# Graph transformer layer pair: where the self-loops, folds and row transposes are done

## Chip, cores and metric

One core of a Trainium2 chip runs the whole program. The metric is the device time of one execution in microseconds; the shown time is the median of three runs. TensorE (PE) runs at one of two clocks, 1.2 or 2.4 GHz, as the chip grants them; the granted clock is given as a share of the higher one. DVE is the vector engine, ACT the scalar engine, POOL is GpSimd, SP the engine that here only issues DMAs.

## What is computed

N = 3125 nodes of width 128, 103,125 directed edges (100,000 drawn, both ways, and 3125 loops), sorted by destination; the layer adds another self-loop for every node. Two layers follow each other, after `h = relu(layernorm(x))`. The reference, cut:

```python
xn = _layernorm(x, ln1_g[l], ln1_b[l])
pos = xn @ Wpos[l] + bpos[l] + deg[:, None] * Wdeg[l][0] + bdeg[l]
xp = xn + pos
q, k, v = xp @ Wq[l] + bq[l], xp @ Wk[l] + bk[l], xp @ Wv[l] + bv[l]     # 8 heads of 16
att = clip(einsum('ehd,ehd->eh', q[dst], k[src]) / scale, -50, 50)       # nan -> 0
ex = exp(att - m[dst]); alpha = ex / segment_sum(ex, dst)[dst]
aggr = segment_sum(v[src] * alpha, dst)
x = x + (aggr @ Wo[l] + bo[l])
x = x + (gelu(_layernorm(x, ...) @ W1[l] + b1[l]) @ W2[l] + b2[l])
```

## The kernel before

Nodes lie in 25 blocks of 128 (partition = node in its block). There are two orders of the blocks: the natural one, and the ranked one (blocks by how many tiles of edges they have), in which both layers work. `NAT` are the 7 batches of four natural blocks (the last has one), `CHUNKS` the 9 chunks of ranked blocks (seven of three, two of two). Edges come in 806 tiles of 128, taken in 202 groups of up to four a layer (6 "seam" groups that touch two blocks a tile, 196 main ones).

**Prelude.** A histogram in 16 steps (`hist_step`) counts degrees: DVE makes one-hot tiles, PE multiplies them. Between its steps PE does other small work: it folds the position weights into Wq, Wk, Wv of both layers (`fold_bias`, `fold_positions`, two matmuls of 384 columns in each, "u" and "fold"), transposes the normalised input (`turn_nat`) and the rows of edge indices (`turn_rows`: k 0 and 1 the destinations, 2 and 3 the sources). Then it makes keys and values of 25 blocks in 13 pairs (`keys_values`), which DVE copies to `kv_nat` (adding the degree term) and SP stores to a table in HBM; then the queries of 7 batches (`queries`). For each batch DVE copies the queries out (`queries_nat`), computes the self-loops' scores (`self_scores`: five instructions, lines 1455 to 1459), and, with ACT, splits the queries into three bf16 parts (`q_first_nat`, `q_rest_nat`, `q_second_nat`, `q_third_nat`; two buffers `q_parts`). ACT takes the exponential (`loop_exp_nat`), DVE multiplies it with the values (`loop_values_nat`). SP moves each block's three parts to its rank in `qp` (L622, one DMA of 96 KB a block). `degT` and `degR` put the degrees in ranked order, at the end of the queries.

POOL gathers rows of the table by edge (L755, one indirect DMA a tile, 128 KB) into a ring of 8 groups, `kvr`. `kv_nat` lies in that ring, so in the first groups POOL waits for the batches of self-loops (`elif 1 <= n <= NATS: pool.wait_ge(s_agg0, n)`).

**Edge phase**, for each layer: in iteration n DVE runs `edge_iteration` (product q*k, L1522; the sums of group n-2 into `agg`, L1549; message of n-1, L1540; scores L1526; clipping L1530 to L1535; one-hot of n+2, L1515), PE `edge_q(n+1)` (L992) and `edge_sum(n-1)` (L1005), ACT the exponentials and the transposed one-hots. One iteration is called a slot here; it lasts from one L1522 to the next. PE's bank 2 holds one group's queries, so `edge_q(n+1)` waits for the product of n.

When a chunk's edges are done, its dense work (`dense_parts`) is spread over the next slots after `BASE[c]` (32, 56, 81, 105, 129, 154, 178, 195, 203): DVE in slot 0 `attention_norm`, 2 `add_to_x`, 4 and so on; in the first layer also the next layer's q, k, v from slot 13 on, whose own self-loops are made from them (`loop_scores` in slot 15, `loop_values` in slot 17). Each engine runs its parts behind its own part of the edge iteration. SP sorted the first layer's finished self-loops into rank order by 25 DMAs in slot 4 (`rank_loops`, L629), and loads the input again from slot 8 (`load_x0`).

Of the kernel before, what the change touches and what calls it, by code (L numbers as in the profile page):

```python
# [113 lines left out]
ROWS_AFTER = {1: (0,), 3: (1,), 5: (2,), 6: (3,)}  # L114
# [6 lines left out]
SP_OUT, SP_TABLE = 10, 15  # L121
SLOTS = BASE[-1] + DVE_Q3 + 1
# [73 lines left out]
def turn_numbers():  # L196
# [9 lines left out]
    for l in range(L):  # L206
        use(0, l, "u", 3 + 2 * l)
    for l in range(L):
        use(0, l, "fold", 7 - l)
# [8 lines left out]
    for c in range(NATS):  # L218
        use(0, c, "q", (1, 4, 5, 6, 7, 3)[c % 6])
    for phase in range(1, L + 1):  # L220
# [29 lines left out]
def build(nc, x_in, src_flat, src_tiles, dst_tiles, dst_last, weights, out):  # L250
    with ExitStack() as ctx:
# [39 lines left out]
        loops_nat = sb("loops_nat", [P, BLOCKS, AGG])  # L291
# [73 lines left out]
        x0 = x_nat = loops_nat[:].rearrange("p b c -> p (b c)")[:, 0:NP].rearrange("p (b c) -> p b c", c=D)  # L365
# [3 lines left out]
        spare = spare[:, 2 * HE:2 * HE + 8 * SC * P].bitcast(F32)  # L369
        step_dst, step_src = (spare[:, k * SC * P:(k + 1) * SC * P].bitcast(I32) for k in range(2))  # L370
        step_dst_f, step_src_f = (spare[:, k * SC * P:(k + 1) * SC * P] for k in (2, 3))
# [7 lines left out]
        spare = hT[:].rearrange("p f c -> p (f c)")  # L379
        wposT = spare[:, 0:L * D].rearrange("p (l c) -> p l c", l=L)  # L380
        wdeg_wide = spare[:, L * D:2 * L * D].rearrange("p (l c) -> p l c", l=L)
        counts = spare[:, 4 * D:4 * D + HI]
# [65 lines left out]
        s_loops_ranked = sem("s_loops_ranked")  # L448
# [78 lines left out]
        def turn_no(phase, c):  # L527

            return NATS + (phase - 1) * NCH + c + 1

# [37 lines left out]
        def _(sp):  # L568
# [55 lines left out]
            def rank_loops():  # L624

                sp.wait_ge(s_agg0, NATS)
                for b0, nb in NAT:
                    for j, r in enumerate(read_block_ranks(ENG.SP, b0, nb)):
                        sp.dma_start(loops[:, bass.ds(r, 1), :], loops_nat[:, b0 + j:b0 + j + 1, :]).then_inc(s_loops_ranked, 16)  # L629

            def load_x0():

                sp.wait_ge(s_loops_ranked, 16 * BLOCKS)
# [24 lines left out]
            for l in range(L):  # L658
                for s in range(SLOTS):
# [15 lines left out]
        def _(pool):  # L675
# [65 lines left out]
            for n in range(L * GROUPS):  # L741
# [9 lines left out]
                elif 1 <= n <= NATS:  # L751
                    pool.wait_ge(s_agg0, n)
# [5 lines left out]
        def _(pe):  # L758
# [26 lines left out]
            def fold_bias():  # L785
# [12 lines left out]
                for l in range(L):  # L798
                    pe.wait_ge(s_wdeg, l + 1)
                    pe.matmul(use(0, l, "u")[:, 0:3 * D], wdeg_wide[:, l, :], w[l][:, W_QKV:W_QKV + 3 * D], start=True, stop=True).then_inc(full(0, l, "u")[0], 1)  # L800

            def fold_positions():
                pe.wait_ge(*read(0, 0, "posT"))
                for l in range(L):
                    pe.matmul(use(0, l, "fold")[:, 0:3 * D], wposT[:, l, :], w[l][:, W_QKV:W_QKV + 3 * D], start=True, stop=True).then_inc(full(0, l, "fold")[0], 1)
# [50 lines left out]
            for k in range(HSTEPS):  # L856
# [6 lines left out]
                elif k == 3:  # L863
                    fold_bias()
                elif k == 4:
                    turn_ranks()
                elif k == 6:
                    fold_positions()
# [10 lines left out]
            for l in range(L):  # L879
                pe.wait_ge(*read(0, l, "fold"))  # L880
# [12 lines left out]
            pe.wait_ge(s_deg, 1)  # L893
            pe.transpose(degT_ps, deg[:, 0, :], ident[:]).then_inc(s_degT_ps, 1)
            pe.wait_ge(s_degT, 1)
# [796 lines left out]
```

## Time and profile before

| | |
|---|---|
| median of 3 runs | 2920.66 us (2920.16 to 2921.53) |
| the profiled execution: time, span | 2918.08 us, 2916.4 us |
| start of keys and values on PE | 108.66 us |
| first gather of layer 1 | 149.74 us |
| first and last issue of the DMAs to qp | 158.88, 191.69 us |
| first edge matmul, first product | 195.25, 199.85 us |
| first product of layer 2 | 1562.8 us |
| mean granted clock of PE | 0.64 |

The difference between the execution's time and its span, 1.7 us, lies around the program. A time of the table is read from the start of the span. Everything before 195.25 us is the prelude; the remaining 2721 us are the two edge phases and their tails.

### The profile page before, as it was taken

What the parts mean: (1) busy time and instruction counts of PE and PEld (TensorE: products, weight loads), DVE (VectorE), ACT (ScalarE), POOL (GpSimd) and SP (SyncE); (2) the same over time, 40 slices, a digit from 0 to 9 for tenths busy, and PEclk for the clock granted to TensorE, in tenths of its full rate; (3) what the DMA queues carried; (4) which work ended last, traced back from release to release, by engine and by line L of the source; (5) the groups of instructions that cost most, each with busy time, mean ns of one, the idle gap of its engine ahead of it and who ended that gap; (6) DMA issues with size and microseconds to landing.
All of it is one profiled execution on the core that took longest, in us unless ns stands there. A gap on an engine that the chain in (4) does not pass through costs nothing.

```text
span 2916.4 us, 39090 instructions
## 1 busy us (share of the span) xinstructions
PE 1839.7 (63%) x9908; PEld 1461.3 (50%) x9908; DVE 1729.1 (59%) x5116; ACT 945.9 (32%) x2192; POOL 1570.4 (54%) x1669
## 2 busy tenths in 40 slices
PE   7956566666666656666673665666565666656666
PEld 6635444544545545454552544555454545545545
DVE  7365565656666666566672555555556656565565
ACT  7122224242333323242442222323232323323233
POOL 5055555555555555555524555565555555555651
PEclk8556657575756657565665755756566665666576
DMA  3144333333333333333322333333333333333331
GB/s 88 58 126 144 107 98 94 111 97 102 103 109 101 103 95 105 103 96 109 102 60 77 112 103 93 104 107 100 107 91 107 103 106 96 108 100 106 106 95 34
DMA packets 123531, 289.01 MB, mean 99 GB/s; under 512 B 31524, under 2 KB 57056, under 8 KB 123328
## 3 DMA queue, kind: packets, MB, share of 16 engines
q0 software_dynamic: 77824, 212.31, 25.4%
q1 hardware_dynamic: 45504, 74.20, 7.7%
q8 instruction: 102, 1.67, 0.2%
q14 instruction: 101, 0.83, 0.1%
HBM read 272.16 MB, written 8.38 MB: 96 GB/s over the span
## 4 chain that ended last, share of the span: by engine, by line
another core or an unknown queue 33%; DVE 29%; issue 17%; PE 17%; DVEq 2%; ACT 2%; SPq 1%; POOL 0%; DMA 0%; ACTq 0%; POOLq 0%
DVE agg L1549 13%; PE bank L1005 5%; PE bank L992 5%; DVE onehot L1515 3%; DVE prod L1522 3%; PE bank L781 2%; DVE attc L1535 2%; DVE msg L1540 1%; DVEq L557 1%; DVE att L1526 1%; DVE attnan L1530 1%; PE bank L842 1%; PE bank L947 1%; PE bank L770 1%
## 5 line engine op out<-in xcount | busy, mean ns | idle before, releaser
L755 POOL DMA_INDIRECT kvr<-kv_table,srcidx x1612 | 1526.2, 947 | 1227.3 <-DVE msg L1540 677.5
L992 PE MATMUL bank<-qp,onehotT 128*128 x4992 | 690.2, 269 | 706.8 <-DVE prod L1522 383.3
L1005 PE MATMUL bank<-msg,onehot 128*128 128x136 f32 x3328 | 817.7, 420 | 310.6 <-DVE msg L1540 310.4
L992 PEld LDWEIGHTS bank<-qp,onehotT 128*128 128x128 bf16 x4992 | 497.9, 103 | 955.7 <-issue 841.4
L1005 PEld LDWEIGHTS bank<-msg,onehot 128*128 128x128 f32 x3328 | 706.7, 304 | 336.2 <-DVE msg L1540 333.7
L1549 DVE TENSOR_TENSOR agg<-agg,bank 128x136 f32 x1628 | 471.6, 290 | 517.2 <-remote 478.2
L1184 ACT ACTIVATE bank<-attc 128x32 f32<-128x32 f32 x404 | 81.2, 201 | 1743.3 <-DVE attc L1535 1481.2
L1522 DVE TENSOR_TENSOR prod<-kvr,bank 128x512 f32<-128x512 f32 x404 | 276.1, 683 | 413.8 <-remote 350.9
L1175 ACT ACTIVATE apart<-relT,minus_p 128x512 bf16<-128x512 bf16 x416 | 293.8, 706 | 0.5
L1515 DVE TENSOR_TENSOR onehot<-bank,rel 128x512 f32<-128x512 f32 x416 | 282.9, 683 | 0.5
L1540 DVE TENSOR_TENSOR msg<-kvr,bank 128x512 f32<-128x512 f32 x404 | 274.4, 679 | 0.7 <-ACT bank L1184 0.5
L1526 DVE TENSOR_REDUCE att<-prod 128x32 f32<-128x512 f32 x404 | 273.6, 677 | 0.1
L1179 ACT ACTIVATE onehotT<-apart 128x512 bf16<-128x512 bf16 x416 | 261.9, 629 | 13.1
L1531 DVE TENSOR_SCALAR attc<-att 128x32 f32<-128x32 f32 x404 | 96.8, 240 | 0.0
L1419 DVE TENSOR_TENSOR x<-x,bank 128x384 f32<-128x384 f32 (+1 forms) x36 | 18.9, 524 | 118.3 <-PE bank L770 55.5
L1187 ACT ACTIVATE msg<-attc 128x32 f32<-128x32 f32 x404 | 86.0, 213 | 0.0
L781 PE MATMUL bank<-kvr 128*128 128x100 bf16 x416 | 76.9, 358 | 11.3 <-DVE kvr L1225 11.3
L1535 DVE COPY_PREDICATED attc<-attnan,zeros 128x32 f32<-128x32 uint8 x404 | 75.1, 186 | 0.0
L1530 DVE TENSOR_TENSOR attnan<-att 128x32 uint8<-128x32 f32 x404 | 74.0, 183 | 0.1
L781 PEld LDWEIGHTS bank<-kvr 128*128 128x128 bf16 x416 | 60.0, 145 | 27.4 <-DVE kvr L1225 12.2
L947 PE MATMUL bank<-w,hT 128*128 128x128 f32 x400 | 68.9, 325 | 3.2 <-issue 2.6
L1184 ACT ACT_TABLE_LOAD x51 | 65.4, 1283 | 0.9
(209 smaller groups left out, 1018.0 us busy)
## 6 DMA issues: line engine op xcount, KB each, us to landing
relT<-rel_table SPq DMA_DIRECT2D x104, 512.0 KB
kvr<-kv_table,srcidx POOLq DMA_INDIRECT x1612
kv_table<-qkv SPq DMA_DIRECT2D x25, 128.0 KB
kv_table<-kvr SPq DMA_DIRECT2D x12, 256.0 KB, 2.1
qp<-hT SPq DMA_DIRECT2D x25, 96.0 KB
loops<-loops_nat SPq DMA_DIRECT2D x25, 68.0 KB
w<-weights SPq DMA_DIRECT2D x2, 840.0 KB, 7.4
loops<-x_in SPq DMA_DIRECT2D x5, 320.0 KB, 5.6
```

The source lines that it names most:

```text
L755: pool.indirect_dma_start(kvr[:, n % RING, j, :], None, kv_table[l], bass.IndirectOffsetOnAxis(ap=srcidx[:, step:step + 1], axis=0)).then_ ...
L781: mm = pe.matmul(counts_ps, oh_low[:, buf, :, :, t].rearrange("p i n -> p (i n)"), oh_high[:, buf, :, :, t].rearrange("p i n -> p (i n)"), ...
L992: mm = pe.matmul(bank[2][:, j * D:(j + 1) * D], onehotT[:, m % OHT, j, :], qp[:, bass.ds(ranks[j + h], 1), part, :].rearrange("p a c -> p ...
L1005: mm = pe.matmul(sum_ps(n, k), onehot[:, m % OH, j, :], msg[:, n % 2, j, :], start=(m, j) == of[0], stop=(m, j) == of[-1])
L1175: act.activation(apart[:], relT[:, m // BODY % 2, r, :], ACT.Abs, bias=minus_p[:]).then_inc(s_apart, 1)
L1179: act.activation(onehotT[:, m % OHT, :, :].rearrange("p j e -> p (j e)"), apart[:], ACT.Relu, bias=1.0, scale=-1.0).then_inc(s_ohT, 1)
L1184: act.activation(ex, attc[:, n % 2, :], ACT.Exp).then_inc(s_ex, 1)
L1515: dve.tensor_tensor(onehot[:, m % OH, :, :], iota_ps.unsqueeze(1).broadcast_to([P, G, P]), rel[:, row:row + G].unsqueeze(2).broadcast_to([ ...
L1522: dve.tensor_tensor(prod[:], kvr[:, n % RING, :, 0:D], bank[2][:].rearrange("p (j c) -> p j c", c=D), ALU.mult).then_inc(s_prod, 1)
L1526: dve.tensor_reduce(att[:, n % 2, :], prod[:].rearrange("p j (h d) -> p (j h) d", d=HD), AX, ALU.add).then_inc(s_att, 1)
L1540: dve.tensor_tensor(by_head(msg[:, n % 2, :, 0:D]), by_head(kvr[:, n % RING, :, D:KV]), ex.rearrange("p (j h) -> p j h", h=H).unsqueeze(3) ...
L1549: dve.tensor_tensor(target, target, sum_ps(n, j), ALU.add).then_inc(s_agg, 1)
```

## The change

1. First layer's self-loops: no longer made in natural order in the prelude, but for each ranked chunk c shortly before its `BASE[c]`. SP loads the chunk's keys and values back from the table (`load_loops`, slot -7, one DMA of 128 KB a block), DVE adds up the three bf16 parts of the queries (`loop1_queries`, slot -4, two additions), computes the scores (slot -3), ACT the exponential (slot -3), DVE the product with the values (slot -2). `rank_loops` and POOL's waits for `s_agg0` go.
2. Second layer's "u" and "fold", and the transposes of the destination rows (`turn_rows` 0 and 1), leave the histogram; PE does them behind the queries, ACT and DVE take them up there; the one-hots of groups 0 and 1 are made there too, behind the queries on DVE.
3. `degT` and `degR` are done among the keys and values (PE behind pairs 6 and 8, DVE behind pairs 2 and 4).
4. Buffers: `x_nat` gets its own memory, `loops_nat` goes; `step_dst_f` lies in `msg`, `wposT` and `wdeg_wide` in `xnT`.

```diff
-ROWS_AFTER = {1: (0,), 3: (1,), 5: (2,), 6: (3,)}
+ROWS_AFTER = {5: (2,), 6: (3,)}
+SP_LOOP1, DVE_LOOP1_Q, DVE_LOOP1_SCORES, ACT_LOOP1, DVE_LOOP1 = -7, -4, -3, -3, -2
...
+            def load_loops(c):
+                b0, nb = CHUNKS[c]
+                blocks = read_perm(ENG.SP, b0, nb)
+                if c >= 2:
+                    sp.wait_ge(s_table[buffer(1, c)], stored(1, c - 2))
+                    sp.wait_ge(s_agg0, loop_no(1, c - 2))
+                    sp.wait_ge(s_r1, turn_no(1, c - 2))
+                    sp.wait_ge(s_q1, turn_no(1, c - 2))
+                table = kv_table[0].rearrange("(b p) c -> p b c", p=P)
+                for j, b in enumerate(blocks):
+                    sp.dma_start(qkv[:, buffer(1, c), j:j + 1, D:3 * D], table[:, bass.ds(b, 1), :]).then_inc(s_loop1_kv, 16)
...
-                    if (l, s) == (0, BODY):
-                        rank_loops()
-                    elif (l, s) == (0, 2 * BODY):
+                    if (l, s) == (0, 2 * BODY):
                         load_x0()
                     for c, at in parts_at(s, LATE_SP):
+                        if l == 0 and at == SP_LOOP1:
+                            load_loops(c)
...
-                elif 1 <= n <= NATS:
-                    pool.wait_ge(s_agg0, n)
...
             for i in range(2, len(KV_PAIRS)):
                 keys_values(i)
+                if i == 6:
+                    pe.wait_ge(s_deg, 1)
+                    pe.transpose(degT_ps, deg[:, 0, :], ident[:]).then_inc(s_degT_ps, 1)
+                elif i == 8:
+                    pe.wait_ge(s_degT, 1)
+                    pe.matmul(degR_ps, degT, placed[:], start=True, stop=True).then_inc(s_degR_ps, 1)
             for c in range(NATS):
                 queries(c)
+            for k in range(2):
+                turn_rows(k)
+            for l in range(1, L):
+                fold_degree(l)
+                fold_positions(l)
...
             def attention_norm(phase, c):
                 if l == 0:
+                    dve.wait_ge(s_loop1, c + 1)
...
+            def loop1_queries(c):
+                nb, u = CHUNKS[c][1], buffer(1, c)
+                q = qkv[:, u, 0:nb, 0:D]
+                dve.tensor_tensor(q, blocks_of(qp[:, :, 2, :], c), blocks_of(qp[:, :, 1, :], c), ALU.add).then_inc(s_loop1_sum, 1)
+                dve.wait_ge(s_loop1_sum, c + 1)
+                dve.tensor_tensor(q, q, blocks_of(qp[:, :, 0, :], c), ALU.add).then_inc(s_loop1_q, 1)
...
             for c in range(NATS + 1):
                 if c < NATS:
-                    b0, nb = NAT[c]
                     queries_nat(c)
-                    self_scores(q_nat[:, c % 2, 0:nb, :], kv_nat[:, b0:b0 + nb, 0:D], b0, nb)
                 if c >= 1:
-                    loop_values_nat(c - 1)
                     q_third_nat(c - 1)
                 if c < NATS:
                     q_rest_nat(c)
+            for k in range(2):
+                dve.wait_ge(*read(0, k, "rows"))
+            edge_onehot(0)
+            edge_onehot(1)
+            for l in range(1, L):
+                fold_positions(l)
+                dve.wait_ge(*read(0, l, "u"))
```

## Rows read from the trace of the kernel before

**Rows 1.** The page's busy time by engine, whole span.

```profile
PE 1839.7 (63%) x9908; PEld 1461.3 (50%) x9908; DVE 1729.1 (59%) x5116; ACT 945.9 (32%) x2192; POOL 1570.4 (54%) x1669
```

**Rows 2.** Stretches of the prelude: bounds, length, busy time by engine, clock, DMA share, GB/s.

```profile
50.00:109.00 59.00, 58.75 (x314) 47.85 (x313) 35.60 (x29) 19.82 (x56) 15.12 (x6) 0.59 0.18 51
109.00:147.00 38.00, 38.00 (x83) 16.13 (x82) 11.68 (x31) 5.78 (x11) 0.00 (x0) 0.50 0.22 76
147.00:195.00 48.00, 24.15 (x78) 15.19 (x77) 34.75 (x89) 10.38 (x22) 29.66 (x30) 0.50 0.48 139
```

**Rows 3.** Timeline of PE in the prelude: start, us, line, tiles, records.

```profile
39.15 2.91 PE L800 MATMUL bank<-w,hT 128*128 128x384 f32 x4
...
56.45 2.78 PE L805 MATMUL bank<-w,hT 128*128 128x384 f32 x4
...
84.15 1.06 PE L824 MATMUL bank<-ident,qp 128*128 128x128 f32 x4
...
91.32 0.85 PE L824 MATMUL bank<-ident,qp 128*128 128x128 f32 x3
...
191.32 0.62 PE L896 MATMUL bank<-placed,xn 25*128 25x25 f32 x2 [20.79 <-issue]
```

**Rows 4.** Timeline of DVE from the queries to the first product.

```profile
147.45 2.48 DVE L1515 TENSOR_TENSOR onehot<-bank,rel 128x512 f32<-128x512 f32 x4
150.56 1.12 DVE L1590 SCALAR_TENSOR_TENSOR qkv<-u_deg,deg,bank 128x128 f32<-128x128 f32 x4 [0.63 <-PE bank L770]
...
158.07 0.68 DVE L1605 TENSOR_TENSOR hT<-qres,hT 128x512 bf16<-128x512 f32 x1
...
199.85 0.69 DVE L1522 TENSOR_TENSOR prod<-kvr,bank 128x512 f32<-128x512 f32 x1 [7.68 <-remote]
```

**Rows 5.** Timeline of SP: all the DMAs to qp, then single batches.

```profile
158.88 33.30 SPq L622 DMA_DIRECT2D qp<-hT  x25
...
158.88 2.54 SPq L622 DMA_DIRECT2D qp<-hT  x4
...
176.07 5.80 SPq L622 DMA_DIRECT2D qp<-hT  x4
...
188.78 2.42 SPq L622 DMA_DIRECT2D qp<-hT  x4
```

**Rows 6.** Timeline of POOL: the first gathers of layer 1.

```profile
149.74 0.99 POOL L755 DMA_INDIRECT kvr<-kv_table,srcidx  x1 [42.88 <-DMA kv_table<-kvr]
...
158.42 1.15 POOL L755 DMA_INDIRECT kvr<-kv_table,srcidx  x1 [3.94 <-DVE loops_nat L1611]
```

**Rows 7.** DVE groups by form: count, busy us, mean ns, idle before.

```profile
L1444 DVE TENSOR_TENSOR qres<-qkv,qp 128x384 f32<-128x384 f32 x7 | 3.8, 549 | 0.0
...
L1458 DVE TENSOR_SCALAR loop_att<-loop_att 128x24 f32<-128x24 f32 x7 | 1.9, 266 | 0.2
...
L1444 DVE TENSOR_TENSOR qres<-qkv,qp 128x256 f32<-128x256 f32 x2 | 0.8, 420 | 0.0
```

**Rows 8.** Timeline of DVE, two slots with edge work alone.

```profile
540.74 0.68 DVE L1522 TENSOR_TENSOR prod<-kvr,bank 128x512 f32<-128x512 f32 x1
...
546.18 0.69 DVE L1522 TENSOR_TENSOR prod<-kvr,bank 128x512 f32<-128x512 f32 x1 [1.72 <-remote]
550.59 0.30 DVE L1549 TENSOR_TENSOR agg<-agg,bank 128x136 f32 x1 [3.72 <-remote]
...
553.54 0.68 DVE L1522 TENSOR_TENSOR prod<-kvr,bank 128x512 f32<-128x512 f32 x1
```

**Rows 9.** Timeline of DVE, a long slot with chunk 2's normalisation behind it.

```profile
732.05 0.69 DVE L1522 TENSOR_TENSOR prod<-kvr,bank 128x512 f32<-128x512 f32 x1 [1.77 <-issue]
...
739.41 0.58 DVE L1409 TENSOR_TENSOR agg<-agg,loops 128x408 f32<-128x408 f32 x1
...
740.84 0.69 DVE L1522 TENSOR_TENSOR prod<-kvr,bank 128x512 f32<-128x512 f32 x1
...
744.85 0.69 DVE L1522 TENSOR_TENSOR prod<-kvr,bank 128x512 f32<-128x512 f32 x1 [0.38 <-PE bank L992]
```

More of the change, by code:

```diff
@@ L205, in turn_numbers @@
     use(0, 0, "bias", 4)
[L206 to L209, printed above, removed]
+    use(0, 0, "u", 3)
+    use(0, 0, "fold", 7)
     use(0, 0, "biasT", 4)
@@ L219, in turn_numbers @@
         use(0, c, "q", (1, 4, 5, 6, 7, 3)[c % 6])
+    for k in range(2):
+        use(0, k, "rows", 4 + k)
+    use(0, 1, "u", 6)
+    use(0, 1, "fold", 7)
     for phase in range(1, L + 1):
@@ L797, in fold_bias, with fold_degree, fold_positions @@
                 mm.then_inc(full(0, 0, "bias")[0], 1)
[L798 to L802, printed above, removed]
+            def fold_degree(l):
+                pe.wait_ge(s_wdeg, l + 1)
+                claim(0, l, "u")
+                pe.matmul(use(0, l, "u")[:, 0:3 * D], wdeg_wide[:, l, :], w[l][:, W_QKV:W_QKV + 3 * D], start=True, stop=True).then_inc(full(0, l, "u")[0], 1)
+            def fold_positions(l):
                 pe.wait_ge(*read(0, 0, "posT"))
-                for l in range(L):
-                    pe.matmul(use(0, l, "fold")[:, 0:3 * D], wposT[:, l, :], w[l][:, W_QKV:W_QKV + 3 * D], start=True, stop=True).then_inc(full(0, l, "fold")[0], 1)
+                claim(0, l, "fold")
+                pe.matmul(use(0, l, "fold")[:, 0:3 * D], wposT[:, l, :], w[l][:, W_QKV:W_QKV + 3 * D], start=True, stop=True).then_inc(full(0, l, "fold")[0], 1)
             def turn_bias():
@@ L878, in _ @@
             pe.wait_ge(s_bias3, 16 * PARTS)
-            for l in range(L):
-                pe.wait_ge(*read(0, l, "fold"))
+            pe.wait_ge(*read(0, 0, "fold"))
             keys_values(0)
@@ L1066, in _, with rows_out @@
             act.copy(bias_parts[:], bank[TURN[0, 0, "biasT"][0]][0:PARTS * L * RC, 0:D]).then_inc(read(0, 0, "biasT")[0], 1)
+            def rows_out(k):
+                act.wait_ge(*full(0, k, "rows"))
+                cols = slice(k % 2 * 4 * P, min(SC, (k % 2 + 1) * 4) * P)
+                act.copy((rel, srcidx)[k // 2][:, cols], bank[TURN[0, k, "rows"][0]][:, 0:cols.stop - cols.start]).then_inc(read(0, k, "rows")[0], 1)
             for c in range(NATS):
@@ L1072, in _ @@
                 for k in ROWS_AFTER.get(c, ()):
-                    act.wait_ge(*full(0, k, "rows"))
-                    cols = slice(k % 2 * 4 * P, min(SC, (k % 2 + 1) * 4) * P)
-                    act.copy((rel, srcidx)[k // 2][:, cols], bank[TURN[0, k, "rows"][0]][:, 0:cols.stop - cols.start]).then_inc(read(0, k, "rows")[0], 1)
+                    rows_out(k)
             act.wait_ge(s_deg_in, 1)
@@ L1142, in dense_parts @@
                     b0, by = CHUNKS[c][0], blocks_by(c)
+                    if phase == 1 and at == ACT_LOOP1:
+                        loop1_exp(c)
                     if at == ACT_OUT:
@@ L1316, in position_bias, with fold_positions @@
                 dve.tensor_tensor(bias_col[:, :, R_QKV:R_QKV + 3], bias_col[:, :, R_QKV:R_QKV + 3], added, ALU.add).then_inc(read(0, 0, "bias")[0], 1)
[L1318 to L1322 removed]
+            def fold_positions(l):
+                dve.wait_ge(*full(0, l, "fold"))
+                dve.tensor_tensor(w[l][:, W_QKV:W_QKV + 3 * D], w[l][:, W_QKV:W_QKV + 3 * D], bank[TURN[0, l, "fold"][0]][:, 0:3 * D], ALU.add).then_inc(read(0, l, "fold")[0], 1)
             dve.wait_ge(s_last, 16)
@@ L1365, in _ @@
             dve.wait_ge(s_deg, 1)
-            for l in range(L):
-                dve.wait_ge(*read(0, l, "u"))
+            dve.wait_ge(*read(0, 0, "u"))
             for i, (b0, nb) in enumerate(KV_PAIRS):
@@ L1576, in _ @@
             dve.wait_ge(s_iota_ps, 1)
-            for k in range(2):
-                dve.wait_ge(*read(0, k, "rows"))
-            edge_onehot(0)
-            edge_onehot(1)
             def queries_nat(c):
```

116 lines of the change are left out of this document (69 added, 47 removed).

## The prediction

> **What bounds the kernel now.** I read the page first. PE is busy 63% of the span and DVE 59% [rows 1], so no engine bounds the whole, and the change must be read by stage: the prelude (to 195 us) and the two edge phases.
>
> In the prelude, the stretches show PE without a gap: busy 58.75 of 59.00 us from 50 to 109, and 38.00 of 38 from 109 to 147 [rows 2]. There PE sets the end, and a matmul taken out is worth its own time. From 147 to 195 no engine is full (PE 24.15 of 48 us). The timeline of DVE shows the first batch's third part made at 158.07, and the timeline of SP shows its 25 DMAs to `qp` beginning right then, at 158.88, and taking 33.3 us [rows 4, 5]. The first product comes at 199.85, after 7.68 us of idle time, about 8 us behind the last of these DMAs. So here SP's queue sets the end, 1.33 us a block. This rate is not constant: a batch of four takes 2.54 us at the start, 2.42 near the end, and 5.80 in between. POOL gathers from 149.74 on, pauses for 3.94 us until 158.42 because of a batch of self-loops, and then gathers on [rows 6]. The slow batch lies deep in that second stretch of gathers, so I read the slow rate as gathers and `qp` transfers contending.
>
> In the edge phase slots alternate. The timeline of DVE shows a short slot, 540.74 to 546.18 (5.44 us, with 1.72 of idle time at its end), and a long one, 546.18 to 553.54 (7.36 us, with 3.72 of idle time in it): 12.80 us for two [rows 8]. DVE has 5.4 us of idle time in such a pair, and waits for PE in both places.
>
> **Part 1, less in the histogram.** "u" and "fold" of both layers take 2.91 and 2.78 us [rows 3]; the second layer's halves are 1.45 and 1.39. The two transposes of destination rows take 1.06 and 0.85, overlapped with their neighbours by about 0.2 each, so 1.5 together. DVE's one-hot tiles are not late for this: it is busy only 35.60 of the 59 us [rows 2]. Sum: keys and values begin 4.3 us sooner. The same work comes back behind the queries (PE 1.45 + 1.39 + 1.9 us, ACT's copies, DVE's 2.48 us of one-hots and a fold of 0.5). PE idles 20.79 us there [rows 3], DVE 7.68 [rows 4], so I cost it at nothing. If `qp` arrived 7 us sooner than I say, about 4 us of it would come onto the path.
>
> **Part 2, `degT` and `degR` among the keys and values.** They are three matmul records on an engine that is full there. `degR` takes 0.62 [rows 3] and the transpose no more than a quarter of 1.06 to 0.4; I take 0.8 us together (bounds 0 and 1.0). DVE waits for them behind pair 2 and again behind pair 4, until PE has done pairs 6 and 8. What queues behind it is copies and SP's stores, and it has 26 of 38 us free [rows 2] to catch up before pair 12. The last store, and so the first gather, moves by PE's shift alone: -4.3 + 0.8 = -3.5 us.
>
> **Part 3, no self-loops in the prelude.** The queries are full 3.5 us sooner. DVE then has 1.12 us of copies and two passes before the first third part, without the five score instructions (about 2 us) and `loop_values`. Its 2.48 us of one-hots ended just before the queries were there (0.63 idle), so moving those gives nothing. I count 147.0 for the first queries, two rounds DVE to ACT and back, and the second batch's copy 3.8 us behind the first (PE's pace): first third part ready at about 152.7, against 158.75. SP starts 6 us sooner.
>
> But POOL no longer pauses: it starts at 146.2 and runs 32 gathers back to back, to about 188. Before, SP's first batches met a queue of gathers that had just begun; now the gathers are 6.5 us ahead when SP starts. What do 25 issues cost then? Bounds: 0.64 us each, the first batch of [rows 5], 16 us in all, and then DVE and PE set the pace; and 1.93 (5.80 over three intervals) until the gathers end near 188, then 0.64. The second gives about 18 + 7 blocks with the loads of ranks between, last issue at 198. Before it was 1.33. I take 1.5 us a block, between before's mean and the slow row, as more of the 25 lie under gathers: 37.8 us, last issue at 190.5 against 192.2, a gain of 1.7 us. The expected 6 us are mostly given back.
>
> The Trainium skill bears on this: DMA: Bandwidth & Descriptors, section "SWDGE vs HWDGE vs iDMA", says that gathers and SP's DMAs run on the same 16 DMA engines, which take turns between the queues. The trace agrees in kind (2.54 and 5.80 us for the same batch). Were the turns equal in bytes, half of the 139 GB/s of [rows 2] would carry a block of 98 KB in 1.4 us; that estimate would end the 25 at 187.8 and the sum would be 2.7 us lower.
>
> **Part 4, self-loops in the edge phase.** A chunk of three blocks adds to DVE two additions, the product, the reduction and the values at 0.55 each, and 0.18 + 0.27 + 0.19 of small ones [rows 7]: 3.4 us over three slots (1.1, 1.8, 0.55). A chunk of two has five at 0.42 and small ones: 2.6. In all 7 x 3.4 + 2 x 2.6 = 29 us.
>
> What of it shows? In a short slot 1.72 us of idle time lie exactly where these parts run [rows 8]. In a long slot nothing is free at that place, but chunk 2's normalisation (1.4 us) was put there: the slot lasts 8.79 us (732.05 to 740.84) and the next 4.01, together 12.80, the same pair [rows 9]. So one insertion of 1.4 us is free in either slot. Three in a row are more: slots of 1.8 and 0.55 on one side and 1.1 on the other exceed what the pair has by 0 to 1.2 us. I take 0.5 a chunk for the seven: 3.5. Chunk 7's parts fall among chunk 6's QKV work: 0.7. Chunk 8's fall in the last three slots, where no long wait is left before the tail: 2 of its 2.6 us. Sum +6.2 us (bounds -4, as a shifted slot can also shorten a pair, and 29). ACT gains 9 short exponentials and loses 7; its table is the one that the edge exponentials use. Its table load now comes before the first edge exponential, while ACT waits for it. SP's 25 loads replace 25 smaller DMAs and have 3 slots (19 us) to land; what they wait for is chunk c-2's, two dozen slots old. At chunk 8 it is one slot old, and then SP holds back at most a load that is needed 4 slots later.
>
> **The sum.** -1.7 (prelude) + 6.2 (edge) = +4.5 us on the profiled execution's own 2918.1 (span 2916.4 and 1.7 around it): 2922.6. That execution lies 2.6 below the median; on the median it is 2925, +0.15%. A difference of 0.2% (5.8 us) is about what can be told from none here.
>
> **Rivals.**
> - *Faster: SP's queue is freed.* If the `qp` DMAs keep a pace of 1.0 us instead of 1.5, the prelude gains 14 us, and with +4.5 or less from the edge phase the time is about 2911. For it: 2.42 and 2.54 us for batches beside running gathers. Against: 5.80 in the long stretch. It decides from 1.1 us a block down.
> - *Slower: the gathers take the DMA engines.* At 1.93 us a block until they end, the last issue comes at 198, 6 us later than before; 2920.7 + 6 + 6.2 = 2933. It decides from 1.6 us a block up, with the edge cost as I have it.
> - *Slower: DVE's added work shows.* If more than half of the 29 us lands on the path: 2934; all of it: 2948. For it: DVE's next product follows its last part at once in long slots. Against: the pair that did not grow [rows 9].
> - *Nothing moves.* The 3.5 us of PE's shift are hidden in SP's queue, the insertions in idle time: 2921; I hold it as part of the forecast's own range.
>
> **How the numbers follow.** Forecast, between 2915 and 2926.5: 0.38. Faster: 0.27. Gathers: 0.20. DVE's work: 0.15. The predicted time is the first case's, 2925. The range 2909 to 2937 takes in the first three and the lesser half of the last. Faster 0.27, same 0.38, slower 0.35, from these cases; the likeliest one's own range is 2915 to 2926.5.
>
> **What the profile after would show.** Keys and values on PE from 104.4 us, queries from 143.1; the first gather at 146.2; the first DMA to `qp` at 152.7 and the 25 in 38 us; the first edge product at 198 (199.85 before). From there to the first product of layer 2, 1363 us before, 6 us more; the slots at `BASE[c]` -4 to -2 longer, their neighbours shorter. Layer 2 the same. I am wrong if the 25 DMAs take under 28 or over 42 us, or if the edge phase of layer 1 grows by more than 12 us or shrinks: its pattern of short and long slots may settle differently after each chunk, which no row here lets me price.

## The result, and the profile after

The changed kernel took 2931.95 us (median of 6 runs, 2928.52 to 2935.12) against 2921.1 us of the kernel before beside it (6 runs, 2920.16 to 2924.35). The ratio is 1.0035, with a 95% interval of 1.0022 to 1.0047: slower by a third of a per cent, just clear of the 0.2% that counts as no change. The forecast was 2925 us in a range of 2909 to 2937, with "no change" as the likeliest case. The time lies in the range, but on the slower side.

The profiled execution of the changed kernel took 2928.52 us (span 2926.7), 10.4 us more than that of before. Stretches of the prelude, to set beside [rows 2] (the last one is new):

```profile
50.00:109.00 59.00, 58.15 (x305) 46.40 (x303) 34.81 (x27) 18.62 (x52) 14.38 (x12) 0.92 0.19 51
109.00:147.00 38.00, 38.00 (x88) 17.03 (x87) 11.64 (x32) 5.78 (x11) 0.00 (x0) 0.50 0.26 86
147.00:195.00 48.00, 25.54 (x77) 15.52 (x77) 11.15 (x28) 5.57 (x9) 30.78 (x32) 0.50 0.39 112
195.00:211.00 16.00, 3.79 (x26) 2.47 (x24) 7.81 (x17) 4.98 (x9) 0.00 (x0) 0.50 0.36 113
```

Up to 147 us the work takes as long as it did (PE 58.15 and 38.00 us, before 58.75 and 38.00). Only the granted clock of the first stretch differs, 0.92 for 0.59, and PE's busy time there hardly follows it. From 147 to 195 VectorE is busy 11.15 us where it was 34.75. Only part of that is work taken out, and the DMAs moved less as well (112 GB/s for 139): everything waits. The timeline of SP, then of VectorE (to set beside [rows 4, 5]) and of GpSimd (beside [rows 6]):

```profile
153.78 51.48 SPq L637 DMA_DIRECT2D qp<-hT  x25
...
159.00 7.24 SPq L637 DMA_DIRECT2D qp<-hT  x4
```

```profile
148.11 1.12 DVE L1667 SCALAR_TENSOR_TENSOR qkv<-u_deg,deg,bank 128x128 f32<-128x128 f32 x4 [3.15 <-PE bank L789]
...
152.96 0.69 DVE L1682 TENSOR_TENSOR hT<-qres,hT 128x512 bf16<-128x512 f32 x1
...
180.31 1.12 DVE L1667 SCALAR_TENSOR_TENSOR qkv<-u_deg,deg,bank 128x128 f32<-128x128 f32 x4 [20.28 <-remote]
...
193.08 1.12 DVE L1667 SCALAR_TENSOR_TENSOR qkv<-u_deg,deg,bank 128x128 f32<-128x128 f32 x4 [10.13 <-remote]
...
210.78 0.69 DVE L1603 TENSOR_TENSOR prod<-kvr,bank 128x512 f32<-128x512 f32 x1 [3.54 <-PE bank L1020]
```

```profile
147.30 1.00 POOL L774 DMA_INDIRECT kvr<-kv_table,srcidx  x1 [43.40 <-DMA kv_table<-kvr]
148.61 0.95 POOL L774 DMA_INDIRECT kvr<-kv_table,srcidx  x1 [0.31 <-issue]
...
186.58 0.95 POOL L774 DMA_INDIRECT kvr<-kv_table,srcidx  x1 [0.30 <-issue]
```

The reader is to see three things. VectorE makes the first third part from 152.96 on and has it at 153.65 (forecast 152.7), and SP starts right behind it. GpSimd gathers 32 times without a pause, 1.25 us apart. And VectorE twice waits for TensorE's query matmuls, 20.28 and 10.13 us ("remote": a signal came, and no instruction's recorded end lies where it could have sent it). TensorE's own timeline shows the same from its side:

```profile
159.00 0.28 PE L789 MATMUL bank<-bias,ones 3*128 3x128 bf16 x1
...
168.39 0.26 PE L789 MATMUL bank<-bias,ones 3*128 3x128 bf16 x1 [0.86 <-issue]
171.19 0.37 PE L845 MATMUL bank<-ident,msg 128*128 128x128 f32 x1 [2.54 <-issue]
...
186.59 0.37 PE L845 MATMUL bank<-ident,msg 128*128 128x128 f32 x1 [4.53 <-issue]
188.80 0.37 PE L845 MATMUL bank<-ident,msg 128*128 128x128 f32 x1 [1.84 <-issue]
```

The first row is the last matmul of queries 3: it is recorded until 159.3, and VectorE gets them at 180.31. Seven transposes that took 1.06 + 0.85 us before [rows 3] now start 2.1 to 4.9 us apart and wait for nothing that the profile shows. This ends some 6 us after the last gather was issued (186.58). The trace also records when each signal (a semaphore's update) is sent. TensorE's for queries 3 is sent at 180.28. The next six, for queries 4, 5 and 6, both transposed rows and "u", are sent together, from 193.06 to 193.39, although queries 4 are recorded until 163.0.

Where the 10.4 us are: the first edge product comes 10.9 us later (210.78 for 199.85). From there to the first product of layer 2 (1572.15, before at 1562.83) it took 1361.4 us against 1363.0, 1.6 less. From there to the end it took 1.1 more.

### The profile page after: what moved, and what is told of

It is laid out like the page before. It is cut to its first block, busy times and chain, and to the rows that moved or that the text cites. A ratio compares the mean times of both kernels' runs of the same rounds, so it can differ in the third digit from the quotient of the medians.

```text
span 2926.7 us, 39204 instructions
## 1 busy us (share of the span) xinstructions
PE 1855.4 (63%) x9908; PEld 1474.0 (50%) x9908; DVE 1743.2 (60%) x5146; ACT 947.4 (32%) x2194; POOL 1574.6 (54%) x1669
## 4 chain that ended last, share of the span: by engine, by line
another core or an unknown queue 33%; DVE 30%; PE 17%; issue 17%; DVEq 2%; ACT 1%; POOL 0%; SPq 0%; DMA 0%; ACTq 0%; POOLq 0%
DVE agg L1630 13%; PE bank L1033 6%; PE bank L1020 4%; DVE onehot L1596 4%; DVE prod L1603 3%; PE bank L800 2%; DVE attc L1616 2%; DVEq L572 2%; DVE msg L1621 2%; DVE att L1607 1%; DVE attnan L1611 1%; PE bank L863 1%; PE bank L789 1%; DVE xn L1443 1%
## 5 line engine op out<-in xcount | busy, mean ns | idle before, releaser
L1612 DVE TENSOR_SCALAR attc<-att 128x32 f32<-128x32 f32 x404 | 84.5, 209 | 0.0
```

## The experiments

Theory G: the gathers, run back to back, hold up TensorE and what waits for it. Rivals: SP's queue is slow by itself; what was moved behind the queries (row transposes, folds) comes late; the self-loops' work shows in the edge phase; the gathers take the DMA engines by their bytes. Ratios are to the kernel before on the same chip, with 95% intervals. The chips differ: the first four kernels ran beside a kernel before of 2921.8 us (35 runs), the next four of 2879.5 us (17), the last four of 2261.0 us (9). Only ratios are compared across these groups, and the first two groups' with the third only with care. The changed kernel as it is was timed in the first pair alone.

**Gathers paced by third parts.** The place of the removed pause, filled again:

```
                 if n >= RING:
                     pool.wait_ge(s_msg, n - RING + 1)
+                elif 1 <= n <= NATS:
+                    pool.wait_ge(s_q3, n)
```

> The changed kernel, with GpSimd's gathers of groups 1 to 7 each waiting for one more third part of the prelude's query chunks (the place where the kernel before had them wait for the self-loops). Theory G (the 32 gathers, back to back from 147.3 us, hold up SP's 25 DMAs and TensorE's queries): the gaps of 20.3 and 10.1 us before queries 3 and 4 on VectorE go, the 25 DMAs take under 40 us instead of 51, the first edge product comes at 190 to 199 us instead of 210.8, and the time is 10 to 18 us under the changed kernel's: 2912 to 2922, no slower than the kernel before. Rival S (SP's queue is as slow whatever GpSimd does, and TensorE's late work is its row transposes and folds): the first product stays within 3 us of 210.8 and the time within 3 us of the changed kernel's.

2915.14 us, ratio 0.9984 [0.9964, 1.0004]. Its timelines of SP and VectorE:

```profile
153.19 22.92 SPq L637 DMA_DIRECT2D qp<-hT  x25
```

```profile
176.15 2.48 DVE L1598 TENSOR_TENSOR onehot<-bank,rel 128x512 f32<-128x512 f32 x4 [0.64 <-ACT rel L1104]
...
193.27 0.69 DVE L1605 TENSOR_TENSOR prod<-kvr,bank 128x512 f32<-128x512 f32 x1 [14.18 <-remote]
```

and TensorE's for the first product:

```profile
179.40 2.82 PE L1022 MATMUL bank<-qp,onehotT 128*128 x24 [8.61 <-issue]
```

With one pause of 1.87 us after the fourth gather (from 153.33 on they run again) the 25 DMAs take 22.92 us instead of 51.48, with gathers beside them nearly all the time, and none of TensorE's signals up to 170.80 is late. The gathers themselves are a little slower there: from 153.33 to 171.82 they start 1.54 us apart in the mean, for 1.25. Which of the two matters, the pause or the slower pace that followed it, this run can't tell. So SP's queue is not slow by itself, and a shared use of the DMA engines is not what cost 1.33 or 2.06 us a block. The first product comes 17.5 us sooner than in the changed kernel, and the time is 0.5% better than the changed kernel's ratio. But it could have come sooner still: VectorE has done everything at 179.1, TensorE's matmuls for it are recorded from 179.40 to 182.2, and the signal is sent at 193.15, when the string of gathers, 1.25 us apart by then, has ended (its last starts at 190.78). Work behind the queries is no cause either: the same transposes and folds ran from 167.09 to 170.8.

**Gathers after the queries.** The changed kernel with

```
                 if n >= RING:
                     pool.wait_ge(s_msg, n - RING + 1)
+                elif n == 1:
+                    pool.wait_ge(s_q3, NATS)
```

> The changed kernel, with all gathers but the first group's four waiting for the last third part of the queries. Theory G: with no gather beside them the query chunks on VectorE run without a gap and the 25 DMAs keep to SP's own rate; the first edge product comes at 185 to 195 us. The 28 gathers then take 35 us from the last third part on, 5 us a group against 6.4 us of a slot, so that VectorE waits in the first slots once for the second group, some 2 to 6 us; the time is 2908 to 2920. Rival S: the first product stays within 3 us of 210.8, and the time is that of the changed kernel or above it by that wait.

2931.18 us, ratio 1.0032 [1.0013, 1.0051]. The prelude did what theory G said (25 DMAs in 21.46 us, first product at 188.79), the time did not. The timeline of VectorE tells why:

```profile
188.79 0.69 DVE L1605 TENSOR_TENSOR prod<-kvr,bank 128x512 f32<-128x512 f32 x1 [11.31 <-remote]
...
214.16 0.69 DVE L1605 TENSOR_TENSOR prod<-kvr,bank 128x512 f32<-128x512 f32 x1 [22.34 <-remote]
```

and TensorE's for the second of these products:

```profile
189.73 2.85 PE L1022 MATMUL bank<-qp,onehotT 128*128 x24 [9.49 <-issue]
```

I had expected a wait of 2 to 6 us for the data of the second group; its four gathers had been issued by 179, and the trace has their data landed at 182.26. What came late was TensorE again: 28 gathers ran from 174.16 to 208.9, and the second group's queries were recorded from 189.73 to 192.6 and signalled at 214.06. The string had been moved onto the edge phase, and cost there what it had cost in the prelude. This miss says most of the theory's content: it doesn't matter which work of TensorE the gathers lie beside, but that it has something to hand over while they run 1.25 us apart.

**No self-loops in the first layer.** The loads, scores, exponentials and values of `loop1_*` are left out, and in `attention_norm`:

```
-                    dve.wait_ge(s_loop1, c + 1)
-                    dve.tensor_tensor(blocks_of(agg, c), blocks_of(agg, c), blocks_of(loops, c), ALU.add).then_inc(s_looped, 1)
+                    dve.tensor_tensor(blocks_of(agg, c), blocks_of(agg, c), ones[:, 0:1].unsqueeze(2).broadcast_to([P, CHUNKS[c][1], AGG]), ALU.add).then_inc(s_looped, 1)
```

> The changed kernel without the first layer's self-loops: no loads of keys and values by rank, no scores, exponentials and values for them, and a constant 1 is added to the sums in their place (so the first layer's attention lacks its self-loops). The prediction's price of the nine chunks is 6.2 us in all: 2925.7 if the changed kernel runs at 2932, 2922 beside a run at 2928.5. The reading of the two traces (1361.4 us from first product to first product against 1363.0 before) gives at most 2 us. A third, that the 29 us of VectorE work shows in full, gives 29 us less. The first edge product is at 210.8 us in all of them.

2931.2 us, ratio 1.0034 [1.0016, 1.0051], against 1.0035 with the loops: nothing that the medians can tell. First product at 210.63, from there to layer 2 1357.3 us, 4.1 less than the changed kernel.

**Parts 1 and 2 alone.** The kernel before with the second layer's folds and the row transposes behind the queries, the ranked degrees among the keys and values, self-loops and their pacing as before; the edit on TensorE (those on the other engines are left out here):

```
             for i in range(2, len(KV_PAIRS)):
                 keys_values(i)
+                if i == 6:
+                    pe.wait_ge(s_deg, 1)
+                    pe.transpose(degT_ps, deg[:, 0, :], ident[:]).then_inc(s_degT_ps, 1)
+                elif i == 8:
+                    pe.wait_ge(s_degT, 1)
+                    pe.matmul(degR_ps, degT, placed[:], start=True, stop=True).then_inc(s_degR_ps, 1)
             for c in range(NATS):
                 queries(c)
+            for k in range(2):
+                turn_rows(k)
+            for l in range(1, L):
+                fold_degree(l)
+                fold_positions(l)
```

> The kernel before with parts 1 and 2 of the change alone: the second layer's folds and the row transposes 0 and 1 behind the queries, the ranked degrees among the keys and values; self-loops still in block order in the prelude, and GpSimd's gathers paced by them. Theory G: VectorE starts the keys and values 2.7 us sooner, nothing is held up, and the first edge product comes at 196 to 199.5 us against 199.85; the time is 0 to 4 us under the kernel before's 2921. Rival S (what was moved behind the queries is what comes late): the first product comes 5 us or more later than 199.85, and the time is 2926 or more.

2917.24 us, ratio 0.9992 [0.9973, 1.0011]. First product at 196.7 (199.85 before), from there to layer 2 1361.2. Parts 1 and 2 do no harm, with all their work behind the queries, and the rival that blames that work falls. Against the paced kernel above, which has part 3 too: first product 196.7 and 193.3, then 1361.2 and 1366.2.

**A lead of three groups.** If strings of gathers are the cost, the ring should not be filled in one go. The changed kernel with

```
-                if n >= RING:
-                    pool.wait_ge(s_msg, n - RING + 1)
+                if n >= 3:
+                    pool.wait_ge(s_msg, n - 3 + 1)
+                elif n == 1:
+                    pool.wait_ge(s_q3, 2)
+                elif n == 2:
+                    pool.wait_ge(s_q3, NATS - 2)
```

> The changed kernel, with GpSimd's gathers never more than 3 groups (12 gathers) ahead of VectorE's messages instead of 8 (32 gathers), in both layers; groups 1 and 2 of the first layer wait for 2 and 5 third parts of the queries. Theory G (TensorE stands still while gathers run back to back, once they have run for some 12 us): the first edge product comes at 180 to 188 us instead of 193.3 in the kernel whose gathers were paced by third parts alone, and the first slot of the second layer, 35.2 us with 32 gathers in a row, falls to 6 to 15 us. The time is 2870 to 2895. Rival L (the lead of 8 groups is needed: a gather of 4 x 1.25 us and its landing do not fit behind a message that is only 3 slots old): slots of 6.4 us grow, and the time is 2930 or more. Rival S (the second layer's first slot is long for a reason of its own, the last rows of its table or the clock): it stays at 35 us and the time at 2905 to 2915.

2844.56 us against 2879.51, ratio 0.9881 [0.9866, 0.9897]. First product at 181.47. At the second layer's start the kernel before (and the changed one, 35.2 us as well) loses more than in the prelude. The timeline of VectorE in the kernel before:

```profile
1562.83 0.69 DVE L1522 TENSOR_TENSOR prod<-kvr,bank 128x512 f32<-128x512 f32 x1 [7.85 <-remote]
...
1598.04 0.69 DVE L1522 TENSOR_TENSOR prod<-kvr,bank 128x512 f32<-128x512 f32 x1 [32.18 <-remote]
```

The trace tells that the second wait is TensorE's: its signal is sent at 1597.94, while the second group's gathered data have landed at 1562.94. The timeline of TensorE there, and below it that of the kernel with the lead of three:

```profile
1563.77 2.86 PE L992 MATMUL bank<-qp,onehotT 128*128 x24 [4.97 <-DVE prod L1522]
1598.97 2.86 PE L992 MATMUL bank<-qp,onehotT 128*128 x24 [32.34 <-DVE prod L1522]
```

```profile
1531.80 2.83 PE L1024 MATMUL bank<-qp,onehotT 128*128 x24 [3.60 <-DVE prod L1607]
1540.43 2.83 PE L1024 MATMUL bank<-qp,onehotT 128*128 x24 [5.80 <-DVE prod L1607]
```

Before, the first slot lasts 35.2 us under 32 gathers in a row; here 8.6 under 12. That is 26.6 us at the second layer's start and 29.3 in the prelude (210.78 to 181.47). Of these 56 us some 45 arrive at the end (1.0035 to 0.9881 of 2920 us); the profile with narrow gathers, from the same chip and with the full lead, shows where others go: the first layer's edge phase is 1349.4 us here and 1343.6 there, and the second layer to its end 1316.0 and 1331.5, only 15.5 less although the first slot alone is 27.9 shorter (8.6 for 36.5). The short lead has a price of its own in the slots behind. It is smaller than the gain, so the rivals L and S fall, on this chip.

**A lead of four groups.** The same with

```
-                if n >= RING:
-                    pool.wait_ge(s_msg, n - RING + 1)
+                if n >= 4:
+                    pool.wait_ge(s_msg, n - 4 + 1)
+                elif n == 1:
+                    pool.wait_ge(s_q3, 2)
+                elif n == 2:
+                    pool.wait_ge(s_q3, 4)
+                elif n == 3:
+                    pool.wait_ge(s_q3, NATS)
```

> The same with a lead of 4 groups (16 gathers, 20 us in a row at the second layer's start); groups 1, 2 and 3 of the first layer wait for 2, 4 and 7 third parts. Theory G: the second layer's first slot ends some 5 us after the string of 16 gathers, so 12 to 20 us against 6 to 15 with a lead of 3, and the time is 2 to 10 us above that kernel's. Rival L: the longer lead is the faster one. Rival S: both have 35 us there.

2853.57 us, ratio 0.9919 [0.9902, 0.9937], 0.4% above the lead of 3. First product at 182.3, the second layer's first slot 14.2 us. The price goes with the length of the string: 12 gathers 8.6 us, 16 gathers 14.2, 32 gathers 35.2 (36.5 in the one run with 32 on this chip).

**The kernel before with a lead of three groups.**

```
-                if n >= RING:
-                    pool.wait_ge(s_msg, n - RING + 1)
-                elif 1 <= n <= NATS:
+                if n >= 3:
+                    pool.wait_ge(s_msg, n - 3 + 1)
+                if 1 <= n <= NATS:
                     pool.wait_ge(s_agg0, n)
```

> The kernel before with the lead of 3 groups (its waits for the self-loops kept). Theory G: its prelude has pauses already, so the first edge product comes at 193 to 200 us against 199.85; the second layer's first slot falls as in the changed kernel, and the time is 2890 to 2900. The changed kernel with a lead of 3 is then 5 to 15 us faster than this one: with the gathers paced, the change pays. Rival: it pays nothing in any case, and the two are within 3 us.

2857.06 us, ratio 0.9924 [0.9911, 0.9936]. First product at 192.44; first layer's edge phase 1345.0 us, against 1349.4 in the changed kernel with the same lead. So with the gathers held short the change pays on this chip: 0.9881 against 0.9924, 12.5 us in the medians. The two profiled executions differ by 5.2 us only: 11.0 gained in the prelude, 4.4 lost in the first layer's edge phase and 1.2 in the second layer. The change's own gain was there; the string of gathers had eaten it.

**Narrow gathers.** Groups 1 to 6 of the first layer gather rows of 64 elements in place of 256 (so these groups work on wrong keys and values), as many gathers as ever:

```
...
+                    cols = 64 if 1 <= n < RING - 1 else KV
+                    rows = kv_table[l].rearrange("n (a c) -> (n a) c", c=cols)
+                    pool.indirect_dma_start(kvr[:, n % RING, j, 0:cols], None, rows, bass.IndirectOffsetOnAxis(ap=srcidx[:, step:step + 1], axis=0)).then_inc(s_kv[n % RING], 16)
```

> The changed kernel, with the gathers of groups 1 to 6 of the first layer moving rows of 256 bytes in place of 1 KB (other rows of the table, so the first six groups of the first layer work on wrong keys and values); GpSimd issues as many gathers as before, back to back. If it is the bytes on the DMA engines that hold TensorE up, the gaps of 20.3 and 10.1 us on VectorE before queries 3 and 4 shrink to a few us and the first edge product comes at 188 to 195 us. If it is GpSimd's issuing itself (1.25 us each, without a pause), they stay, and the first product stays at 205 to 212 us.

2890.49 us, ratio 1.0034 [1.002, 1.0048]: as the changed kernel. The first row is this kernel's stretch of the gathers, the second is the changed kernel's.

```profile
147.00:188.00 41.00, 23.00 (x73) 14.39 (x73) 9.34 (x23) 4.94 (x8) 30.23 (x32) 0.50 0.28 74
```

```profile
147.00:188.00 41.00, 23.01 (x73) 14.44 (x73) 9.34 (x23) 4.95 (x8) 30.78 (x32) 0.50 0.44 128
```

74 GB/s in place of 128, and VectorE still waits 18.79 and 12.21 us, the 25 DMAs take 51.36 us, the first product comes at 210.37. So it is not the gathers' bytes, as rows of a quarter of the size in 24 of the 32 gathers leave the waits nearly where they were.

**Four on a third chip.** The last four ran on a chip that does the kernel before in 2261.0 us. The first is the kernel of the lead of three groups again, with no edit of its own.

> The kernel of the lead of 3 groups again, to stand on the same chip as the three that follow. Its ratio to the kernel before was 0.9881; all theories expect that again, within 0.002.

2338.5 us, ratio 1.0344 [1.0318, 1.0371]. It is 3.4% slower than the kernel before there, where it had been 1.2% faster. All theories missed. The views below show waits from 400 to 1300 us (total, times, longest): the three largest of VectorE in the kernel before, in the profile of the first pair, and then, from this kernel on the third chip, those of VectorE and GpSimd.

```profile
DVE agg L1549 <- remote: 141.9, 44, 4.4
DVE prod L1522 <- remote: 96.4, 35, 5.7
...
DVE qkv L1437 <- remote: 28.4, 5, 6.2
```

```profile
DVE prod L1607 <- DMA kvr<-kv_table,srcidx: 88.7, 64, 4.6
POOL kvr L778 <- DVE msg L1625: 64.5, 46, 3.8
...
DVE x L1467 <- PE bank L793: 41.0, 15, 8.2
DVE qkv L1487 <- PE bank L793: 33.2, 23, 3.3
```

In the first, 291 us of 900 are VectorE's waits marked "remote" (with 24.6 at `x`); on the third chip there is not one. A slot is 5.1 to 5.3 us long there, the four gathers of a group take 5.0 of it, and the chain that ended last lies on GpSimd for 39% of the span. So the 64.5 us that GpSimd waits for messages are lost time there; in the kernel before of the first pair it had 242.4 us of such waits while something else set the pace. The kernel with pauses below shows this on the same chip: it keeps the lead of 8 groups, has 4.9 us of such waits, slots of 5.0 us, and takes 1055.2 us from first product to first product against 1109.7 here. That the short lead is the whole of the 3.4% is argued, not shown: neither the changed kernel as it is nor a profile of the kernel before was run on that chip.

**The lead of three, without the first layer's self-loops.** The two edits above together; a constant 1 is added in the self-loops' place.

> The changed kernel with a lead of 3 groups and without the first layer's self-loops (a constant 1 is added to the sums in their place, so its attention lacks them): the price of part 3's work in the edge phase where no string of gathers disturbs the start. The prediction's term of 6.2 us gives 6.2 us under the kernel with the loops; the two profiles with and without them that exist (1361.4 and 1357.3 us from first product to first product) give 4 us; VectorE's 29 us in full would give 29 us. First edge product at 181 us in all of them.

2331.68 us, ratio 1.0323 [1.0299, 1.0346], against 1.0344: 6.8 us in the medians, with intervals that overlap. In the profiles, first product to first product, 1104.6 us against 1109.7.

**The lead of three, parts 1 and 2 alone.** That kernel with the edit of the kernel before with a lead of three groups.

> Parts 1 and 2 alone (self-loops in block order in the prelude), with a lead of 3 groups and the waits for the self-loops. The kernel before with that lead has its first edge product at 192.4 us and was 12.5 us slower than the whole change with it. The prediction's steps: parts 1 and 2 are worth 2.5 us of it (first product at 189 to 190.5 us), and part 3 takes the rest of the prelude's gain, 8 us, and gives 4 to 6 us back in the edge phase; so this kernel is 2 to 9 us above the whole change with the lead. Rival: parts 1 and 2 bring the whole gain, and the two are within 1 us.

2338.6 us, ratio 1.0363 [1.0341, 1.0385]. The first product comes at 189.7 (181.6 with part 3); parts 1 and 2 are worth 2.7 us against the 192.4 of the kernel before with that lead, as forecast (that kernel ran on the second chip; the changed kernel with this lead has its first product at 181.5 and 181.6 on the two). The totals are equal within their spread (2323 to 2346 and 2329 to 2348), so part 3's 8 us cannot be seen in them on this chip. Nor do single profiles help: from first product to first product this one took 1088.2 us and the one with part 3 1109.7, a difference of 21.6 us, but the two were their kernels' fastest and slowest executions.

**Pauses of GpSimd.** The lead stays at 8 groups; after each of a layer's first seven groups of gathers GpSimd fills a spare tile five times, 2.87 us.

```
+                if g < RING and g > 0:
+                    for i in range(PAUSES):
+                        pool.memset(pause[:], 0.0).then_inc(s_pause, 1)
+                        pool.wait_ge(s_pause, (l * (RING - 1) + g - 1) * PAUSES + i + 1)
```

> The changed kernel with the lead of 8 groups as it was, but GpSimd fills some 3 us with five fills of a spare tile after each group of four gathers before the steady state, in both layers. Theory G in the form that it is the missing pause that holds TensorE up: 5 us of gathers and 3 us without are as good as the steady state's 5 of 6.4, no wait of over 5 us on VectorE is left, the first edge product comes at 180 to 192 us, the second layer's first slot takes 7 to 12 us, and the ratio to the kernel before is 0.985 to 0.992. Rival P (GpSimd busy with anything at all holds TensorE up): first product at 205 us or later, second layer's first slot over 35 us. Rival N (the number of gathers ahead counts, not their pace): the second layer's first slot stays above 25 us.

2293.43 us, ratio 1.0143 [1.0124, 1.0163], where 0.985 to 0.992 was expected. First product at 182.5, second layer's first slot 7.8 us, as theory G says. But this tells nothing apart, for behind the pauses the gathers run from 202 to 1179 us without one (1.25 us apart), and no signal of TensorE is late in all that time. Waits from 400 to 1170 us, no gap before a gather over 0.3 us:

```profile
POOL kvr L781 <- issue: 181.9, 597, 0.3
...
DVE qkv L1490 <- PE bank L796: 29.4, 21, 3.3
...
DVE agg L1637 <- PE bank L1040: 22.7, 43, 1.3
...
POOL kvr L781 <- DVE msg L1628: 4.9, 16, 0.3
```

So theory G does not hold on this chip, and whether it is the pause or the number of gathers that helps on the others stays open. The pauses themselves cost here: the second layer's first eight slots take 60.5 us, against 43.1 with a lead of 3 and no pauses. Where the rest of the 32 us against the kernel before goes stays open.

## Why the prediction came out as it did

- **The total, +4.5 us: inside the range, in part by luck.** The prelude was forecast at -1.7 us and came out at +10.9; the first layer's edge phase at +6.2 and came out at -1.6. The two misses go opposite ways.
- **Part 1 and 2, -3.5 us: right in kind, a little large.** Part 1 was forecast at -4.3 and gave -2.75 (keys and values from 105.91 on, before 108.66), part 2 at +0.8 and took 0.3 (queries from 144.17, before 146.62). VectorE has the first queries at 148.11 (150.56 before, -2.45), the first gather is at 147.30 (149.74, -2.44). With a lead of 3 groups on both, the first product moved by 2.7, across two chips. What was moved behind the queries cost nothing, once the string was gone.
- **Part 3, SP starts 6 us sooner: right** (153.78 for 158.88, -5.1; the third part ready at 153.65, forecast 152.7).
- **Part 3, 1.5 us a block: this step failed.** "The slow batch lies deep in that second stretch of gathers, so I read the slow rate as gathers and `qp` transfers contending." Measured were 2.06 us a block, 51.5 us against 37.8 and against the 42 that I had named as the limit. (At 1.5 us a block the 25 come to 37.5; the prediction wrote 37.8.) The reading was wrong in its mechanism, too. The gathers were the cause, but not by their bytes: with rows of a quarter of the size nothing changed, and with one pause put back the same DMAs ran beside the gathers at 0.92 us. SP was slow mainly because its third parts came late, since VectorE waited for TensorE: between its second batch's last start and its third batch's first lie 16.8 us, and 6.3 between the third and the fourth. The rest is its own slow pace beside the gathers, 2.2 us from one DMA to the next in two batches. I had costed TensorE's part at "nothing" since it idles 20.79 us there. It idled, but its signals didn't pass. The 7.68 us before the first product of [rows 4] bore the mark of it: "remote", as did both waits of [rows 8]; I read them as TensorE's ordinary time. The signals that ended the two waits of [rows 8] were sent 1.8 and 4.1 us after the recorded end of their matmuls.
- **Part 4, +6.2 us: right in size, 4 to 5 measured.** Three pairs of profiles with and without the insertions, first product to first product: 4.1 (no loops), 5.0 (paced against parts 1 and 2 alone), 4.4 (lead 3, changed against before). On the third chip one pair gives 5.1 and the other 21.6, and the executions of each kernel with the lead of three spread over 17 to 23 us, so neither counts for much. No medians show the term clear of their spread. VectorE's 29 us hardly show, as the row of [rows 9] said. That the changed kernel's phase was 1.6 us shorter than before's is not the part's doing: before's profile took 1.8 more than that of parts 1 and 2 alone, whose edge work is the same. The clause "I am wrong if it shrinks" named a sign that one profile of each can't carry.
- **Layer 2 "the same": right (+1.1), and a chance missed.** Its first slot is 35.2 us long in both kernels. The wait of 32.18 us at its start lay in the trace of before all the time.
- **The rivals.** The slower one, "the gathers take the DMA engines", gave 2933 and the last issue at 198 (measured 2931.95, and 204.8). Its time and its place were right and its mechanism wrong, so the time is luck; nor does its 198 follow from its terms: 18 blocks at 1.93 us and 7 at 0.64 take 39.2 us and end at 191.9, and no row shows the other 6 us. The Trainium skill's rule (DMA: Bandwidth & Descriptors, section "SWDGE vs HWDGE vs iDMA") of DMA engines that take turns is neither borne out nor refuted here: with 74 GB/s in place of 128 the prelude took as long, so no run shows a turn that was waited for.

## What to carry to other kernels

A wait that paces an engine can be worth more than the work that it waits for: when an edit takes it away, ask what that engine now does without a break, and look in the trace for a place where it already does so (here the second layer's start, 32 gathers and a stall of 32 us). An idle engine is not a free one where its waiters' rows say "remote": compare when its signal was sent with when its work is recorded to end. And a gain that is tied to a late signal should be timed on more than one chip: the lead of three groups with the change takes 1.2% off the kernel before on one and adds 3.4% on another.

## What the runs showed of the hardware that was not expected

- In the first pair of runs and on two of the three chips of the experiments TensorE's results are signalled late while GpSimd issues gathers 1.25 us apart: queries 3 were recorded until 159.3 and signalled at 180.3 in the changed kernel; the second group's queries of layer 2 were recorded until 1566.6 and signalled at 1597.9 in the kernel before. When it sets in differs: in the changed kernel a signal due 8.2 us after the first gather is on time and one due at 12.0 is late, at layer 2's start in the kernel before one due at 6.0 is already 3.9 us late, and with the gathers at 1.54 us in the paced kernel none is late for 17 us. SP's DMAs are then 2.2 us apart (7.24 us for four, above) where 2.54 us for four is their own pace [rows 5]. The bytes gathered don't matter (74 and 128 GB/s moved). What it is that the gathers hold isn't shown by any row: the granted clock is 0.50, the lower level, in the stretch with and without the stall ([rows 2], and the changed kernel's), and the trace records instructions' own loads as DMAs and has none from 1563 to 1598 us in the kernel before.
- The late signals are no matter of the strings alone. From 400 to 1300 us, with pauses between the groups of four gathers, the signal of a group's queries is sent over 1 us after the recorded end of its matmuls in 72 of 123 recorded cases in the kernel before, by up to 6.2 us, and in 63 of 115 with the lead of three on the second chip. On the third chip none of 161 is late by more than 0.02 us. How much of the 660 us between the chips this makes was not tried.
- On the third chip gathers ran back to back for 976 us and nothing was late. TensorE's granted clock was 0.71 to 0.75 over the span there, 0.61 to 0.66 on the others, and the kernel before took 2261 us instead of 2921. Whether clock and late signals have one cause was not tried.
